# A fused attention and quantized-network layer: the last heads projected without a transfer, a GELU called early, and a re-drawn order

## What is computed

```
x = x + layernorm(attention(layernorm(x)))       # 16 causal heads of 16 channels
x = x + layernorm(network(layernorm(x)))
attention: qkv = lora_linear(x); softmax(q k' / 4, causal) v; lora_linear(...)
network, for blk in 0, 1, 2:
    y = gelu(layernorm(qlora_linear(h)) * g + b)
    h = qlora_linear(y) + h                      # 256x256 weights, 4 bit, LoRA rank 32
```

## Time and profile before

| | |
|---|---|
| median of 3 runs | 1248.01 us (1245.55 to 1249.2) |
| profiled execution | 1250.09 us |
| its span | 1248.3 us |
| mean granted TensorE clock | 0.989 |
| TensorE, ScalarE busy | 1202.1 us, 1095.4 us |
| VectorE, POOL busy | 770.1 us, 435.0 us |

### The profile page before, as it was taken

One profiled execution on the slowest core, in us unless ns is written; L12 is line 12 of the kernel. 1 busy time (PEld: TensorE's weight loads), 2 busy tenths in 40 slices (PEclk: granted clock), 3 DMA queues, 4 the chain that ended last, 5 costly groups with the idle time before them and its releaser, 6 DMA issues.

```text
span 1248.3 us, 29297 instructions
## 1 busy us (share of the span) xinstructions
PE 1202.1 (96%) x10981; PEld 499.3 (40%) x10981; DVE 770.1 (62%) x1904; ACT 1095.4 (88%) x1251; POOL 435.0 (35%) x1373
## 2 busy tenths in 40 slices
PE   8999999999999999999999999999899999999967
PEld 6556434333333333333333333333333333333346
DVE  6775225566657667665674554675677666656466
ACT  4765999999999999999999999999899998999822
POOL 3221235442334444322462132245323145222144
PEclk9999999999999999999999999999899999999979
DMA  5985544554443544454544333456344354432100
GB/s 165 311 312 179 181 138 121 163 175 123 123 136 109 167 137 135 123 149 131 152 142 119 107 108 118 109 151 169 113 121 121 88 151 139 122 103 56 43 14 18
DMA packets 163246, 166.78 MB, mean 134 GB/s; under 512 B 91782, under 2 KB 125084, under 8 KB 163100
## 3 DMA queue, kind: packets, MB, share of 16 engines
q1 hardware_dynamic: 158812, 160.61, 43.8%
q10 hardware_dynamic: 4288, 4.26, 1.1%
HBM read 121.29 MB, written 39.32 MB: 129 GB/s over the span
## 4 chain that ended last, share of the span: by engine, by line
PE 51%; DVE 12%; POOL 7%; SPq 6%; DMA 5%; issue 4%; ACT 4%; DVEq 0%; POOLq 0%; ACTq 0%
PE O L1517 23%; PE S L1499 16%; PE F L209 10%; ACT probs L1442 4%; SPq L595 3%; DMA feed_mem<-turns 3%; DMA qkv_mem<-turns 2%; DVE stC L1611 1%; SPq L1357 1%; DVE feed_mem L1727 1%; DVE feed_mem L1728 1%; POOL tmpC L1390 1%; POOL tmpC L1391 1%; DVE feed_mem L1758 1%; SPq L1354 1%
## 5 line engine op out<-in xcount | busy, mean ns | idle before, releaser
L1442 ACT ACTIVATE probs<-S 128x1024 f32<-128x1024 f32 x1056 | 993.3, 1036 | 57.9 <-PE S L1499 52.7
L1517 PE MATMUL O<-probs,vg 128*32 128x512 f32 (+3 forms) x4608 | 537.7, 566 | 6.6 <-DVE o_turned L1675 3.1
L1499 PE MATMUL S<-q_op,k_op 64*128 64x512 f32 (+3 forms) x2304 | 377.6, 420 | 3.5 <-ACT probs L1442 2.4
L1499 PEld LDWEIGHTS S<-q_op,k_op 64*128 64x128 f32 x2304 | 178.8, 185 | 314.1 <-ACT probs L1442 250.3
L1517 PEld LDWEIGHTS O<-probs,vg 128*32 128x32 f32 x4608 | 112.7, 109 | 215.0 <-issue 192.0
L1420 POOL TENSOR_SCALAR_AFFINE_SELECT probs<-probs 128x512 f32<-128x512 f32 (+1 forms) x160 | 89.8, 572 | 164.0 <-ACT probs L1442 163.6
L1390 POOL TENSOR_SCALAR tmpC<-mvC 128x2 f32<-128x2 f32 x84 | 26.6, 316 | 301.2 <-DVE rstdC L1620 299.6
L209 PE MATMUL F<-wfT,feed_mem 128*32 128x256 f32 x960 | 62.4, 382 | 6.9 <-DVEq L1660 3.9
L1429 POOL TENSOR_TENSOR feed_mem<-feed_mem 128x512 f32<-128x512 f32 x30 | 32.2, 1073 | 104.9 <-DVE feed_mem L1716 104.8
L1758 DVE TENSOR_SCALAR feed_mem<-feed_mem,rstdC,nmrC 128x256 f32<-128x256 f32 x80 | 34.7, 475 | 55.1 <-POOL nmrC L1401 54.2
L1727 DVE SCALAR_TENSOR_TENSOR feed_mem<-feed_mem 128x512 f32<-128x512 f32 x90 | 63.2, 703 | 4.6 <-DVE feed_mem L1736 0.8
(11 more groups left out here) (212 smaller groups left out, 1257.9 us busy)
## 6 DMA issues: line engine op xcount, KB each, us to landing
k_op<-qk_rows SPq DMA_DIRECT2D x256, 256.0 KB, 3.7
qk_rows<-parts SPq DMA_DIRECT2D x32, 512.0 KB, 5.3
q_op<-qk_rows SPq DMA_DIRECT2D x128, 128.0 KB, 3.0
turns<-feed_mem SPq DMA_DIRECT2D x200, 64.0 KB, 1.9
feed_mem<-turns SPq DMA_DIRECT2D x50, 256.0 KB, 2.9
k_op<-qk_rows SPq DMA_DIRECT2D x48, 128.0 KB, 2.6
turns<-qkv_mem SPq DMA_DIRECT2D x80, 64.0 KB, 1.9
qkv_mem<-turns SPq DMA_DIRECT2D x20, 256.0 KB, 3.1
```

The lines of the kernel that those rows point to most:

```text
L1442: nc.scalar.activation(probs[:, n % NP, :, :], S[:, n % NS, :, :], ACT.Exp, scale=SCALE).then_inc(exp_ok, 1)
L1499: last = nc.tensor.matmul(S[:, n % NS, a, at:at + TT - q0], k_op[mine, c % RING, pair, k0:k0 + P], q_op[mine, v % QS, pair, q0:TT], start= ...
L1517: last = nc.tensor.matmul(O[h * STRIP:(h + 1) * STRIP, q0:TT], vg[:, kb, col:col + STRIP], probs[:, n % NP, a, at:at + TT - q0], start=fir ...
```

## The change

The last visit's heads are no longer moved. `project` of the last tile has four pieces per quarter. The bias and channels 0 to 127 stay. Piece n = 2 multiplies only the 64 rows of visit 30 in `attT` by the first 64 rows of the second weight half. Piece n = 3 multiplies `o_div` as it lies, 128 rows, by `w_padded`: the last 64 rows of the weights at the heads' places, with zero rows between. `w_padded` is cleared by VectorE at the start and filled by four transfers of SyncE ahead of the first half's store. ScalarE calls one `Gelu` on a single column that nobody reads, ahead of its first item that is neither an exp nor a GELU. The planner's items follow, and seven of its constants change.

```diff
-FEED_FROM, FEED_EACH = 20.0, 54.0
-BATCH, THIRD, SLACK, BACKLOG = 3, 0.2, 0.3, 9
+FEED_FROM, FEED_EACH = 24.0, 58.0
+BATCH, THIRD, SLACK, BACKLOG = 3, 0.3, 0.5, 9
-GELU_WAIT = 4.0
+GELU_WAIT = 2.0
-SWITCH = {"score": 0.21, "strips": 0.13, "full": 0.2}
+SWITCH = {"score": 0.26, "strips": 0.15, "full": 0.2}
...
-        return NC + lead(name)
+        return NC + lead(name) + (name == "project")
...
-        item(("moved", v), "SP", 2.5, [("divide", v)] + [("project", t - AS, k, pieces("project", t) - 1) for k in range(2) if t >= AS], LAST[v])
+        if v < len(VISITS) - 1:
+            item(("moved", v), "SP", 2.5, [("divide", v)] + [("project", t - AS, k, pieces("project", t) - 1) for k in range(2) if t >= AS], LAST[v])
-    item(("moved_late", len(VISITS) - 1), "ACT", 1.2, [("divide", len(VISITS) - 1)], 0)
...
-            found += [("moved", 4 * t + i) for i in (0, 1, 2, 3) if n >= 1 + i // 2] + ([("moved_late", 4 * t + 3)] if n >= 2 else [])
+            found += [("moved", 4 * t + i) for i in (0, 1, 2) if n >= 1 + i // 2] + ([("divide", 4 * t + 3)] if n > NC else [])
...
+                        if t == 0 and k == 0:
+                            sp.wait_ge(early_out, 1)
+                            sp.wait_ge(pad_ok, 1)
+                            for h in range(HG):
+                                sp.dma_start(w_padded[h * STRIP:h * STRIP + D, :], g["wpT"][HALF + h * D:HALF + (h + 1) * D, NC - 1, :]).then_inc(padded, 16)
...
+                table_called = False
                 for x in order["ACT"]:
+                    if x[0] != "exp" and not x[0].startswith("gelu") and not table_called:
+                        table_called = True
+                        nc.scalar.activation(table[:, :], minus_half[:, 0:1], ACT.Gelu)
...
-                    if x[0] == "moved_late":
-                        move(act, x[1], range(HG // 2, HG))
-                        continue
...
-                        if n:
+                        if n > NC:
+                            pe.wait_ge(o_ready, len(VISITS))
+                            pe.wait_ge(padded, 16 * HG)
+                        elif n:
                             for s in range(2):
-                                pe.wait_ge(moved[s], 16 * HG * (2 * t + n))
+                                pe.wait_ge(moved[s], 16 * HG * (2 * t + (n if s == 0 else 1)))
...
+                        elif t == NT - 1 and name == "project" and n > NC:
+                            last = product(into[:, 0:C], o_div[:, (len(VISITS) - 1) % 2, at], w_padded[:, :], start=False, stop=True, skip_group_check=True)
+                        elif t == NT - 1 and name == "project" and c:
+                            last = product(into[:, 0:C], attT[0:HALF, t % AS, c, at], g["wpT"][0:HALF, c, :], start=False, stop=False, skip_group_check=True)
...
+                nc.vector.memset(w_padded[:, :], 0.0).then_inc(pad_ok, 1)
```

More of the change, by code:

```diff
@@ L1200, in attend_and_feed @@
         o_div = sb("o_div", [P, 2, TT])
+        w_padded = sb("w_padded", [P, C])
+        padded, pad_ok = sem("padded"), sem("pad_ok")
         attT = sb("attT", [P, AS, NC, TT])
@@ L1211, in attend_and_feed @@
         halved = sb("halved", [P, 2 * BLK * NC])
-        minus_half = sb("minus_half", [P, 1])
+        minus_half, table = sb("minus_half", [P, 1]), sb("table", [P, 1])
         S = ctx.enter_context(nc.psum_tensor("S", [P, NS, 2, TT], F32))
@@ L1340, in _ @@
                     elif x[0] == "moved":
-                        move(sp, x[1], range(HG) if x[1] < len(VISITS) - 1 else range(HG // 2))
+                        move(sp, x[1], range(HG))
                     elif x[0] == "x_load":
```

## The result

The changed kernel takes 1270.5 us (median of four), the kernel before 1248.4 beside it on the same chip: a ratio of 1.018 [1.016, 1.020]. It is 22 us slower where I forecast 5.2 us faster, and lies outside the range. The tail did what was forecast; the long stretch ahead of it, for whose order I had taken 0 ± 3.5 us, lost 26.8.

What follows compares the result with a forecast made beforehand. TensorE and ScalarE were taken as near full in the long stretch, latency as deciding the tail; 2.4 + 1.3 + 1.5 + 0 = 5.2 us off the 1248.0 median gave 1242.8 us, range 1237.5 to 1248.5.

Steps and rivals of the forecast that it cites:

- The tail: From the last exp to the end: the last tile's projection and network, latency-bound, forecast to give 5.2 us.
- Its first term: Tail's opening: no transfer for the last visit, so the product starts earlier; 2.4 us, bounds 1.9 and 2.85.
- the VectorE work that the prediction named: Tail's opening: VectorE's work on the previous tile's last half may delay the first statistics, making the gain 1.9 us.
- The early GELU and the clock behind it: Tail's first GELU: table load moved into idle time, 1.3 us; TensorE's clock then staying up, 1.5 us more.
- within 0.3 us: Sign at the tail's opening: the first padded product starts this soon after the end of `o_div`, against 3 us.
- the wait that I gave as their cover: Tail's opening: TensorE's wait for `o_div` hides the added products; without it they would cost 1.5 us.
- For the order I take 0, with bounds of 3.5 us either way from the rounds: Long attention stretch: the planner's new constants were taken to change nothing on balance, within 3.5 us.
- the 0.36 us of the prediction: Long stretch: cost on TensorE of one entry and return between scores and weighing; some 400 rounds carry about 150 us.
- met once or twice more: Rival in the long stretch: repeated stalls at 2.8 us each, 3 to 5 us lost, gain eaten; chance 0.16.
- The later due times bind little: Long stretch: the feed already runs late against old and new due times, so moving them matters little.
- a cover of 10.5 us: End of the stretch: last feed residual precedes last exp by this; rival of late feed or new stall, chance 0.09.
- The prices do not become truer: Planner's switch prices: measured 0.23 to 0.24 and 0.12 to 0.13, against new 0.26 and 0.15.

Runs made afterwards that it cites:

- `tail_only`: The changed kernel with all seven planner constants set back, keeping the projection without a transfer and the early GELU: 1241.6 us, ratio 0.995.
- `after_light`: The changed kernel with ten of the twelve instructions of POOL's root left out for all tiles but the last (computes something else): 1237.5 us.
- `tail_light`: New tail and old order, with ten of the twelve instructions of POOL's root left out for all tiles but the last (computes something else): 1228.8 us.
- `new_feed`: The new tail with the old planner constants, except the feed's due times at 24 and 58: 1268.4 us, ratio 1.017.
- `list_only`: The kernel before with the seven new planner constants and nothing else: 1274.2 us, ratio 1.020.
- `old_switch`: The changed kernel with the old prices of a switch, 0.21 and 0.13: 1249.0 us, ratio 1.001.
- `pow_after`: The changed kernel with POOL's root made in seven instructions, a power and one Newton step: 1240.4 us, ratio 0.993.
- `pow_tail`: New tail and old order, with POOL's root made in seven instructions, a power and one Newton step: 1232.1 us, ratio 0.985.

## Why the prediction was wrong

**The tail: right.** Forecast 5.2 us, measured 5.1 after and 5.3 in `tail_only`. Its first term came out at its lower bound, 1.9 instead of 2.4. In `tail_only` the VectorE work that the prediction named would have done that; in the changed kernel VectorE is idle there, and it is TensorE's added products. The early GELU and the clock behind it together gave 3.3 us of the rest against 2.8: the pause as forecast, the 16 instructions 1.04 us shorter in `tail_only` than without the early GELU (1.54 than before), and the products behind them, for which I had added nothing, 0.6 us. The granted clock stays up there in the changed kernel, as I had taken it to (windows of TensorE):

```profile
1233.00:1235.00 2.00, 1.45 (x11) 1.00 0.00 0
1235.00:1237.00 2.00, 2.00 (x18) 1.00 0.00 0
```

That the product begins "within 0.3 us" of `o_div` was wrong, 1.02 us: the two of the added products that stand there did not fit in the wait that I gave as their cover. Each holds TensorE for some 0.62 us, where I had reckoned 0.5.

**The step that failed: "For the order I take 0, with bounds of 3.5 us either way from the rounds".** It measured -26.8 us. The bounds came from the number of rounds of score and weighing alone. The rounds did fall, by a tenth, and at the 0.36 us of the prediction that would be 16 us of TensorE's time. TensorE's busy time rose by 10.4 us all the same. Even where the clock hardly falls, fewer rounds save nothing that the busy time shows: it is 1043.14 us with 403 entries in `after_light` and 1041.03 with 449 in `tail_light`. What sets the stretch's length is which inputs are there when the fixed order reaches for them, and I had priced that with one observed stall of 2.8 us, "met once or twice more". Idles of ScalarE of 0.7 to 3.7 us came a dozen times more often. And a stall costs twice, a term that I had put at nothing in the stretch: TensorE falls to 1.2 GHz at it. The stretch of the changed kernel has seven such pieces, that of before one (windows of TensorE, first the changed kernel: length, busy us, granted clock, DMA share, GB/s):

```profile
364.00:368.00 4.00, 4.00 (x35) 0.57 0.42 114
589.00:593.00 4.00, 3.45 (x28) 0.57 0.91 298
674.80:678.20 3.40, 3.40 (x29) 0.50 0.00 0
691.90:695.30 3.40, 3.40 (x26) 0.50 0.30 66
889.80:896.70 6.90, 6.66 (x42) 0.51 0.22 74
964.90:968.30 3.40, 3.40 (x32) 0.50 0.06 14
1026.40:1033.20 6.80, 5.21 (x34) 0.50 0.22 45
```
```profile
882.70:889.50 6.80, 4.75 (x32) 0.50 0.31 79
```

Each lies at a pause of TensorE of 1.3 to 4.0 us. By the clock records of the two traces TensorE is busy at that level for 28.8 us of the stretch against 4.8 before. My estimate from these: at full clock the 24.0 us more would have taken half, so some 12 us, as much as TensorE's busy time rose.

**"The later due times bind little": wrong.** `new_feed` changes these alone and loses 26.8 us; in its profiled run the rest is 14.5 us longer. The prediction reckoned with the 8 to 24 us by which the first tiles' dues move; the last due of the last pair moves by 32 counts (398 to 430) of two score units each, some 64 us. The last half starts when lanes and dues let it, and a cover of 10.5 us was too thin to call the dues slack.

**"The prices do not become truer": true, and no help.** Truer or not was the wrong question. All twelve other sets of constants that ran with the new tail were slower than `tail_only`, by 7.4 to 54.5 us; the six that stand one or two constants from the old ones by 8.2 to 54.5. (Cheaper prices ran only together with the other new constants.) The order of before is one out of many that the planner gives, and better than all the others that ran. The expected change of a newly drawn order was not 0 with a narrow spread but a loss; the 15.5 us of large ScalarE idles in 1064 us showed how little it could still win.

**The cause.** Shown: the loss is the order's (`tail_only`, `list_only`); it is idle time of ScalarE behind stalls; and about 20 of 29 us of the difference between the orders disappear when POOL's root is cut, by either of two ways. The plan has the root at 3.1 us, against 3.8 in the mean and 6.1 at the most. In both orders the late root is there. The new order meets it where cuts or feed inputs wait behind it, as at 690 us. Argued, not shown: why the new order meets it more often, and that it is the excess over the planned price that costs, and not the length itself. With a short root only these two orders ran, so for the other losing orders the cause is open; `old_switch` has the longest roots in the mean, 4.0 us, and loses only 7.4 us.

**Open.** 5 to 11 us of the gap in the stretch remain with a short root. A part of it may be the shorter `GELU_WAIT`: in `pow_after` ScalarE still waits 5.2 us directly for the input of a tanh and in `after_light` 6.1, in `pow_tail` and `tail_light` not at all. A short root with the old `GELU_WAIT` in this order was not run.

```profile
ACT feed_mem L1455 <- DVE feed_mem L1736: 5.2, 3, 3.6
```

One stall of the changed kernel is led by a transfer, not by POOL:

```profile
672.58 0.73 DVE L1732 TENSOR_SCALAR feed_mem<-feed_mem,halved 128x256 f32<-128x256 f32 x2 [4.62 <-DMA feed_mem<-turns]
...
674.40 0.76 PE L209 MATMUL F<-wfT,feed_mem 128*32 128x256 f32 x8 [2.75 <-DVEq L1675]
675.93 2.86 ACT L1453 ACTIVATE probs<-S 128x1024 f32<-128x1024 f32 x3 [3.53 <-PE S L1507]
```

VectorE waits 4.62 us for a feed transfer, TensorE then for VectorE, and ScalarE for TensorE. How much of the remainder is of this kind was not tried. A plan drawn with a measured root price was not tried either.

## What to carry to other kernels

An order made by a list scheduler is a draw: change any constant and price it as a new draw, with the spread of its neighbours, not by the size of the constant. Where two engines are near full, a latency chain that is late for some of its instances (here 3.1 us planned and up to 6.1 taken) costs an amount that depends on the order: 9.5 us in one, 30.0 in the other. Test a local edit with the order held fixed first, as `tail_only` does, and look for a latency under which more than one order suffers; shortening it gave more than any order did.

## What the runs showed of the hardware

POOL's small instructions have no fixed length. In the chain at 682 us an instruction on 128x2 takes 0.73 us (682.00, line 1398) and others of the same shape take 0.20. The long ones lie beside a VectorE instruction that reads two tensors (timelines of VectorE, then POOL):

```profile
681.99 0.69 DVE L1744 SCALAR_TENSOR_TENSOR feed_mem<-feed_mem 128x512 f32<-128x512 f32 x1
...
683.97 0.69 DVE L1743 SCALAR_TENSOR_TENSOR feed_mem<-feed_mem 128x512 f32<-128x512 f32 x1
684.70 0.69 DVE L1744 SCALAR_TENSOR_TENSOR feed_mem<-feed_mem 128x512 f32<-128x512 f32 x1
```
```profile
684.21 0.51 POOL L1404 TENSOR_SCALAR tmpC<-tmpC 128x2 f32<-128x2 f32 x1
684.80 0.65 POOL L1405 TENSOR_TENSOR tmpC<-tmpC 128x2 f32<-128x2 f32 x1
685.53 0.22 POOL L1406 TENSOR_SCALAR tmpC<-tmpC 128x2 f32<-128x2 f32 x1
```

Over the changed kernel's 84 roots, 117 of the 1008 instructions take over 0.4 us (up to 0.93), and every one of them overlaps a VectorE instruction with two tensor inputs; the 766 that overlap none take 0.38 us at the most. A chain of twelve such instructions takes 3.2 us at its shortest and 6.1 at its longest. The Trainium skill ("GPSIMD Engine Reference", Specifications) says that the engine shares its SBUF interfaces with VectorE, with contention when VectorE reads two SBUF inputs; these rows agree.

The power instruction on 128x2 took 0.70 to 1.45 us in `pow_tail`, 0.83 in the mean, where I had expected 0.56.

A stall also costs TensorE's clock: the windows in the section before show 1.2 GHz at seven pauses of 1.3 to 4.0 us. Ahead of the piece from 674.80 on, which ran at 1.2 GHz throughout, the clock was full and TensorE little busy (length, busy us, granted clock, DMA share, GB/s):

```profile
671.00:674.80 3.80, 1.05 (x16) 1.00 0.20 70
```

The mean over the stretch is 0.99 in the changed kernel and 1.00 in the kernel before, in `tail_only` and in all four kernels with a short root.
